# Moving the broadcasts of places from GpSimd's queue to SP's, with the places stored in eight copies

## The reference, cut to what matters

```
h = maximum(layernorm(x), 0)                                  # x: 6250 nodes x 64
x = x + segment_sum(h[src], dst, num_segments=6250)           # 200000 edges, sorted by dst
h = maximum(layernorm(x), 0)
for l in range(3):                                            # second layer: attention masks on the same edges
    mask = clip(sigmoid(mlp(x_l[src], x_l[dst])) * 1.5 - 0.45, 0, 1)
    x_l  = segment_sum(mask * d_inv_sqrt[src] * d_inv_sqrt[dst] * x_l[dst], src)
    out  = out + x_l
```

## Time and profile before

| | |
|---|---|
| time, median of 3 runs | 4300.82 us (4297.33 to 4306.86) |
| the profiled execution: its time | 4298.2 us |
| its span in the trace | 4296.5 us |
| sorting stage, first to last store of bins | 71.8 to 498.2 us |
| building stage, first broadcast issued to the next stage's first instruction | 523.8 to 1153.6 us |
| busy share of the span: PE, DVE, ACT, POOL | 87%, 84%, 46%, 55% |
| bytes moved | 794.22 MB, of these 78.69 MB by GpSimd's queue |

### The profile page before, as it was taken

The page is one execution under the profiler, slowest core; times in us unless marked ns, Lnnn a source line. Parts: engine busy times, 40 slices in busy tenths (PEclk is TensorE's granted clock), DMA queues, the critical chain, the costliest instruction groups (busy, mean ns, idle before and its releaser), DMA issues. The chain is left out here.

```text
span 4296.5 us, 257308 instructions
## 1 busy us (share of the span) xinstructions
PE 3754.2 (87%) x99727; PEld 3555.5 (83%) x99728; DVE 3612.2 (84%) x5865; ACT 1965.7 (46%) x5107; POOL 2355.7 (55%) x3286
## 2 busy tenths in 40 slices
PE   5888678888689999799988999799997999979997
PEld 4777577887569999788868999788885999978887
DVE  8999867787758888899966888799995888879998
ACT  5888767777621111555541111255552111135554
POOL 3777523333223333789962333399894333359987
PEclk8888799999889999899989999899998999989999
DMA  1000189999637776566626777566662777756665
GB/s 31 2 2 2 35 282 327 323 330 321 217 131 248 249 248 225 150 171 171 171 72 217 247 247 247 175 173 171 172 170 79 246 247 247 247 151 170 170 171 138
DMA packets 521189, 794.22 MB, mean 185 GB/s; under 512 B 61718, under 2 KB 461514, under 8 KB 521098
## 3 DMA queue, kind: packets, MB, share of 16 engines
q1 hardware_dynamic: 500714, 714.25, 52.5%
q0 software_dynamic: 20384, 78.69, 6.7%
HBM read 672.34 MB, written 120.42 MB: 185 GB/s over the span
## 5 line engine op out<-in xcount | busy, mean ns | idle before, releaser
L1547 POOL TENSOR_TENSOR message<-message 128x448 f32<-128x448 f32 x1029 | 1244.7, 1242 | 195.9 <-ACT message L1531 195.9
L1243 PE MATMUL pre_ps<-rows_a,hotT_a 128*128 128x64 bf16 x21609 | 1302.6, 194 | 55.0 <-DMA hotT_a<-hot_scratch 27.8
L1243 PE MATMUL pre_ps<-table,hotT_a 128*128 128x64 bf16 x21609 | 1301.7, 194 | 1.8 <-issue 1.8
L1243 PEld LDWEIGHTS pre_ps<-rows_a,hotT_a 128*128 128x128 fp8e4 x21609 | 1130.4, 98 | 81.4 <-issue 64.4
L1243 PEld LDWEIGHTS pre_ps<-table,hotT_a 128*128 128x128 fp8e4 x21609 | 1132.8, 98 | 0.8 <-issue 0.7
L1558 DVE TENSOR_TENSOR message<-message 128x448 f32<-128x448 f32 x1029 | 993.5, 966 | 69.3 <-POOL message L1547 69.3
L1359 DVE SCALAR_TENSOR_TENSOR weighed<-pre_ps,w 128x448 f32<-128x448 f32 x1029 | 642.3, 624 | 279.8 <-PE pre_ps L1243 192.8
L1531 ACT ACTIVATE message<-high_ps,mask 128x64 f32<-128x64 f32 x3087 | 699.7, 326 | 248.2 <-PE high_ps L1490 231.2
L1502 PE MATMUL sum_ps<-message,hot_b 128*128 128x192 bf16 x7203 | 783.9, 247 | 6.1 <-DVE message L1558 5.7
L1490 PE MATMUL low_ps<-table,hot_b 128*128 128x64 bf16 x12348 | 529.3, 193 | 152.9 <-issue 62.4
L1490 PEld LDWEIGHTS low_ps<-table,hot_b 128*128 128x128 fp8e4 x12348 | 473.1, 98 | 195.0 <-issue 181.9
(11 more groups left out here) (160 smaller groups left out, 5142.8 us busy)
## 6 DMA issues: line engine op xcount, KB each, us to landing
hotT_a<-hot_scratch SPq DMA_DIRECT2D x1029, 224.0 KB, 4.5
hot_b<-hot_scratch SPq DMA_DIRECT2D x1029, 224.0 KB, 2.7
hot_scratch<-hot SPq DMA_DIRECT2D x343, 336.0 KB, 7.8
hot_a<-hot_scratch SPq DMA_DIRECT2D x147, 784.0 KB, 5.0
places<-slots_scratch POOLq DMA_DIRECT2D x196, 224.0 KB, 6.8
places<-slots_scratch POOLq DMA_DIRECT2D x98, 336.0 KB, 7.2
out<-res SPq DMA_DIRECT2D x1, 1536.0 KB
slots_scratch<-bins SPq DMA_DIRECT2D x49, 16.0 KB, 1.4
```

The lines of the kernel that those rows point to most:

```text
L1243: last = nc.tensor.matmul(pre_ps[g][:, j, :], hotT[:, b, g, end, j * P:(j + 1) * P].bitcast(FP8), table, start=end + part == 0, stop=end = ...
L1547: pool.tensor_tensor(message[:, g, :, 1, :], message[:, g, :, 0, :], top[:, g, :, 0, :, 1], ALU.subtract).then_inc(s["rest_ready"], 1)
```

## The change

Four things change. The scratch tensor of places becomes eight copies of itself, and the sorting stage stores each block's 16 KB eight times, once into each copy. In the building stage GpSimd issues nothing; SP issues the broadcasts, between its stores: after the store of a chunk's last unit it issues the two loads of that chunk for the row two later, without a wait of its own. The source of a load is now all eight copies of a row, each read by 16 partitions, where before it was the one copy read by 128. And since SP issues loads after every chunk's last unit, also in the last pair of rows, it loads two rows more than before (rows 49 and 50, which no unit reads), and waits for these at the end of the stage.

```diff
-                    act.wait_ge(stored[b], nth * 16)
+                    act.wait_ge(stored[b], nth * (16 * COPIES))
...
-                    sp.dma_start(k.slots_dram[:, bass.ds(c, 1), :].rearrange("r c e -> r (c e)"), bins[:, b, :])\
-                        .then_inc(stored[b], 16)
+                    for copy in range(COPIES):
+                        sp.dma_start(k.slots_dram[copy, :, bass.ds(c, 1), :].rearrange("r c e -> r (c e)"), bins[:, b, :])\
+                            .then_inc(stored[b], 16)
...
+    last_of = {z - 1: c for c, (a, z) in enumerate(chunks)}
...
-            @block.gpsimd
-            def _(pool):
+            @block.sync
+            def _(sp):
                 def load(c, h, r):
                     a, z = chunks[c]
                     for e in range(2):
-                        tile = k.slots_dram[bass.ds(r + e * k.HALF, 1), a * G:z * G, :]
-                        pool.dma_start(places[:, h, e, a * G * P:z * G * P],
-                                       tile.rearrange("r c e -> (r c e)").partition_broadcast(P))\
+                        tile = k.slots_dram[:, bass.ds(r + e * k.HALF, 1), a * G:z * G, :]
+                        n = (z - a) * G * P
+                        sp.dma_start(places[:, h, e, a * G * P:z * G * P],
+                                       tile.rearrange("o r c e -> o (r c e)").unsqueeze(1).to_broadcast([COPIES, P // COPIES, n]))\
                             .then_inc(places_in[c][h], 16)
 
-                for c in range(len(chunks)):
-                    load(c, 1, 0)
-                for c in range(len(chunks)):
-                    load(c, 0, 1)
-                for c, (a, z) in enumerate(chunks):
-                    wait_count(pool, s, s["hotT"], z)
-                    load(c, 1, 2)
-                with pool.Fori(1, (NB - 1) // 2) as i:
-                    for c, (a, z) in enumerate(chunks):
-                        for h in range(2):
-                            wait_count(pool, s, s["hotT"], NG + (i - 1) * (2 * NG) + 2 * (z - 1) + h + 1)
-                            load(c, h, i * 2 + 1 + h)
-
-            @block.sync
-            def _(sp):
                 def store(recent):
                     n = recent[0]
                     wait_count(sp, s, s["hotT"], n.u + 1)
                     wait_count(sp, s, s["hot_ready"], n.u + 1)
                     sp.dma_start(k.hot_dram[bass.ds(n.r, 1), :, n.g, :, :].rearrange("r p a b -> (r p) a b"),
                                  hot[:, n.slot, 0:3, :]).then_inc(stored[n.slot], 16)
+                    if n.g in last_of:
+                        load(last_of[n.g], n.h, n.r + 2)
+
+                for c in range(len(chunks)):
+                    load(c, 1, 0)
+                for c in range(len(chunks)):
+                    load(c, 0, 1)
                 each_unit(sp, k, 1, store)
+                for c in range(len(chunks)):
+                    for h in range(2):
+                        sp.wait_ge(places_in[c][h], 32 * (NB // 2 + 1 + h))
                 for g in range(NG):
                     sp.wait_ge(stored[g], 16 * NB)
...
-    k.slots_dram = nc.dram_tensor("slots_scratch", [2 * k.HALF, k.NB, P], U8).ap()
+    k.slots_dram = nc.dram_tensor("slots_scratch", [COPIES, 2 * k.HALF, k.NB, P], U8).ap()
```

More of the change, by code:

```diff
@@ L16 @@
 PARTS = 3
+COPIES = 8
 CH = 8
@@ L498, in _ @@
                 for b in range(2):
-                    sp.sem_inc(stored[b], 16)
+                    sp.sem_inc(stored[b], 16 * COPIES)
                 def row(c, b, nth, first):
                     wait_count(sp, s, s["bins_ready"], c + 3)
-                    sp.dma_start(k.slots_dram[:, bass.ds(c, 1), :].rearrange("r c e -> r (c e)"), bins[:, b, :])\
-                        .then_inc(stored[b], 16)
+                    for copy in range(COPIES):
+                        sp.dma_start(k.slots_dram[copy, :, bass.ds(c, 1), :].rearrange("r c e -> r (c e)"), bins[:, b, :])\
+                            .then_inc(stored[b], 16)
                 each_row(sp, NB, row)
-                sp.wait_ge(stored[0], 16 * (NB // 2 + 2))
-                sp.wait_ge(stored[1], 16 * (NB // 2 + 1))
+                sp.wait_ge(stored[0], 16 * COPIES * (NB // 2 + 2))
+                sp.wait_ge(stored[1], 16 * COPIES * (NB // 2 + 1))
             @block.vector
```

## The result

The changed kernel takes 4411.74 us (median of 4 runs, 4408.9 to 4414.36), against 4299.61 of the kernel before beside it: a ratio of 1.0258, 95% interval 1.024 to 1.0275. It is slower by 112 us, where +108 was forecast (4409, range 4325 to 4520). The profiled execution has a span of 4408.5 us, 112.0 more than before.

What follows compares the result with a forecast made beforehand. The building stage was taken as bound by the VectorE-TensorE-ScalarE round trip, DMA close behind. Sorting 0, GpSimd 0, SP 0 and building +108 gave 4406 us profiled, 4409 as the median, range 4325 to 4520.

Steps and rivals of the forecast that it cites:

- the round trip of 1.69 us a unit: Building stage: paced by the round trip between VectorE, TensorE and ScalarE, 343 units, 580 us, with DMA close behind.
- Eight engines, the term that decides: Building stage: loads run on always the same eight DMA engines, 17.6 MB each, 738 us against 629.8, +108; chance 0.85.
- The reading of the 106-partition store: Kernel's last store: DMA share 0.16 read as two engines, the number dividing 106, so eight copies give eight engines.
- The price of an engine: Building stage: a busy engine moves 24.0 GB/s, between 22.1 (+171 us) and 26.0 (+51 us).
- The two useless rows: Building stage: two more rows loaded, 3.2 MB over eight engines, 17 us of the 108.
- The seven more stores a block: Sorting stage: eight stores take SP 2.7 us of 8.9 a block, hidden, taken as 0.
- the other end: Sorting stage: the cost of the extra stores, taken as 0, could at its other end be about 1 us.
- GpSimd's issues: Building stage: 294 issues, 211.7 us busy, go from GpSimd; gain 0 to 2 us, taken as 0.
- SP's issue of a load: Building stage: 0.332 us each, 26 issues take 8.6 us of a turn of at least 23.7; SP keeps up, 0.
- VectorE's waits: Building stage, sign of the forecast: VectorE idle for DMA ahead of line 984 some 140 us rather than 34.
- the first one: Building stage rival: all sixteen engines carry the loads and waits for stores go; 4271 us, chance 0.09.
- The third rival: Building stage: sixteen engines but one in-order queue, loads ahead of stores; +27 us, 4328, chance 0.03.

Runs made afterwards that it cites:

- swap16: Changed kernel with the loads' source dimensions exchanged to [16 repeats][8 copies][bytes]; 4283.86 us against 4307.77 for the kernel before, ratio 0.9945.
- sixteen: Changed kernel with sixteen copies in place of eight, copies still outermost; 4281.58 us against 4323.51 for the kernel before, ratio 0.9902.
- stores_only: Kernel before plus the sorting stage's eight stores a block; GpSimd still issues and reads only the first copy; ratio 1.0006 to the kernel before.
- pool_swap: Kernel before with eight copies stored, GpSimd still issuing, all eight read as [16 repeats][8 copies][bytes]; ratio 0.9928 to the kernel before.
- swap16_no_extra: Changed kernel with source dimensions exchanged to [16 repeats][8 copies][bytes] and no two useless rows; ratio 0.9918 to the kernel before, 0.9896 when run again.
- queue_only_no_extra: Changed kernel with one copy, plain broadcast issued by SP, and no two useless rows; 4283.42 us, ratio 0.9911 to the kernel before.
- no_extra: Changed kernel without the two useless rows, SP's last pair issuing no loads; ratio 1.0214 to the kernel before.
- four: Changed kernel with four copies in place of eight, source [4 copies][32 repeats][bytes]; 4776.0 us against 4307.77 for the kernel before, ratio 1.1084.

## Why the prediction was right

**What bounds the kernel.** That the stage runs at the round trip of 1.69 us a unit, with DMA close behind, was right. swap16 has no waits for stores; its 600 to 1100 window has 440 VectorE instructions, finds and adds in a ratio of two to one, so 293 units in 500 us, 1.71 each.

**Eight engines, the term that decides.** Shown by three readings. While broadcasts run alone, from 528 to 531, the share is 0.25 for four engines, 0.48 for eight, and 0.98 and 1.05 for sixteen (sixteen and swap16). The time follows the divisor: 1.1084, 1.0258, and 0.9945 or 0.9902. And exchanging two dimensions of the source, with nothing else touched, takes the loss away. The reading of the 106-partition store carried over to a source whose destination has 128 partitions, though it was thin ground: a share of 0.16 is 2.5 engines, not two.

That the eight are always the same is not seen directly, since no view names an engine. It follows from the share later on:

```profile
600.00:1100.00 500.00, 381.94 (x9970) 365.02 (x9968) 333.41 (x357) 332.08 (x510) 0.00 (x0) 0.91 0.73 273
```

Two fifths of a unit's bytes are places and three fifths its store. Each of a fixed eight then carries 0.4/8 + 0.6/16 = 8.75% of all bytes, and each of the others 3.75%. Eight engines full and eight at 3.75/8.75 = 0.43 make a share of 0.71; 0.73 is measured. With eight that change from load to load every engine would carry the same, and nothing would hold the share down while stores are waited for. The same sum gives 0.45 for four engines, against 0.47. It also answers whether TensorE's lower clock is a cause: with eight engines full all the time, the stage can't be waiting for TensorE. No run holds the clock fixed to show this apart.

**The price of an engine.** 24.0 GB/s was taken between 22.1 and 26. Measured: 17.6 MB in 746.6 - 4 us, 23.7 GB/s over the stage. From 600 to 1100 alone it is 8.75% of 273 GB/s, 23.9. The building stage came to +116.8 us where +108 was forecast. At 23.9 the 17.61 MB take 737 us, so of the 9 us some 3 are the rate, and 6 are the ends of the stage, which take nearly 10 us and not 4. That 24.0 was so close is in part luck. The ground for a faster engine counted two engines in the last store, 17.5 GB/s each; by its share of 0.16 there are 2.5, 14.0 GB/s each, no faster than the 13.6 before it. At 22.1 or 26 the same sum gives 4472 or 4352 us. That the whole came within 3 us is luck as well: the rest of the kernel, which the change doesn't touch, gave 4.8 us back: 1.0 more up to the first broadcast, 5.8 less behind the stage (3142.9 before, 3137.1 after). In the other traces that last part lies anywhere between 3134.7 and 3144.1 us, so it belongs to the execution, not to the change.

**The two useless rows.** Their 17 us were in the sum, but I had placed them nowhere. The trace puts most of them at the end: SP stands 10.8 us when all computing is done. In that wait the last microseconds are slower than eight engines would be:

```profile
1259.00:1269.00 10.00, 0.00 (x0) 0.00 (x0) 0.22 (x1) 0.00 (x0) 0.00 (x0) 0.56 0.34 133
...
1265.00:1268.00 3.00, 0.00 (x0) 0.00 (x0) 0.00 (x0) 0.00 (x0) 0.00 (x0) 0.50 0.10 38
```

A share of 0.10 is as much as one or two engines of sixteen. Most likely these still have work when the others of the eight are done, but the views don't name them. The mean of eight engines is thus a little too kind a measure for the end of the stage.

**Costed at nothing.** The seven more stores a block: stores_only has 1.0006. The first broadcast is issued at 523.3 to 523.8 in the three traces with one copy and at 523.6 to 526.5, mostly near 525, in the eight with eight copies; so about 1.5 us are lost ahead of the stage, near the 1 us named as the other end. SP's part was put too low: stores follow each other by 0.53 us, not by the 0.337 of one issue (the last block's eight start from 499.9 to 503.6), so eight take 4.2 us of 8.9 and sixteen nearly all of it. GpSimd's issues: right that they cost nothing as such, since pool_swap keeps them and can't be told from swap16_no_extra, run with it (0.9928 and 0.9918, the intervals overlap). SP's issue of a load: put at 332 ns from the stores, measured 663, twice too low, with no effect, since SP had room.

**VectorE's waits.** Forecast some 140 us for DMA; measured 113.6 for stores and 9.5 for places, and another 10.5 at the stage's end. With 18.9 us more for `add_up` these are 112 of the stage's 116.8. The landing of stores was to grow over 10 us and is 10.2. GpSimd is busy 259 us less in the page (2355.7 to 2096.5), not 212: 44 of it lie in the sorting stage, where its small operations show other durations and nothing waits for them.

**The rivals.** The price of the first one, 4271 or 30 us less, was nearly right for a kernel that uses all sixteen engines: swap16 is 24 us faster than the kernel before it. One of its grounds was half right. The packets of the software queue do cost more a byte, 43% from 600 to 1100 in the kernel before; in pool_swap, with eight copies read, it is 21%, and the waits for stores are gone. So about half of it went with the single copy (queues from 600 to 1100, the kernel before and pool_swap: packets, MB, share of the engines). On SP's queue the single copy cost no time that could be told.

```profile
q1 hardware_dynamic: 40593, 96.98, 49.7%
q0 software_dynamic: 16640, 64.24, 47.0%
...
q1 hardware_dynamic: 42159, 100.75, 53.2%
q0 software_dynamic: 17286, 66.79, 42.6%
```

The third rival, stores delayed by loads ahead of them in one queue, is refuted by swap16, where a store lands in 5.4 us rather than 7.8.

**A faster version.** swap16_no_extra beats both kernels: 0.9918 (0.9905 to 0.9932) in one set of runs and 0.9896 (0.9881 to 0.9911) in another, 31 to 45 us under the kernel before. queue_only_no_extra, which needs no copies, is at 0.9911 and can't be told from it, and pool_swap, which keeps GpSimd's queue and reads eight copies, is at 0.9928. So either half of the change, the queue or the copies, gives the gain, and both together give little or nothing more.

## What to carry to other kernels

Look at the outermost dimension of both sides of every transfer that SP issues before anything else: with four or eight there, four or eight of sixteen DMA engines carried it here, and a transfer that is itself hardly waited for still delayed another that shares its engines. Put a repeat dimension of sixteen outside and the eight copies inside, or have sixteen copies. When a stage's DMA share falls while its time grows, compare the share with the fraction of engines (0.25, 0.48) in a window in which only the suspected transfer runs. Set the window by the first issue, some 3 us behind it: from 526 to 529 the changed kernel shows 0.44, and no_extra, with the same loads issued 1.3 us later, 0.21.

## What the runs showed of the hardware that was not expected

- On GpSimd's queue a broadcast from one copy to 128 partitions costs about a sixth more of the engines' time than one from eight copies (6.9% of the span in stores_only against 5.9% in pool_swap, for the same 20384 packets), and moved the time by 0.8% (1.0006 against 0.9928). On SP's queue one copy and eight gave the same time (0.9944 and 0.9945) and differed in landing, 6.7 and 5.1 us. While broadcasts run alone it is the other way round on both queues: 366 and 353 GB/s from one copy, 241 and 252 from eight, the engines full in all four (from 528 to 531). Why, and why the two queues differ in time, was not found.
- The same source form, eight outermost, takes eight engines on SP's queue and isn't held to the same eight on GpSimd's (share 0.48 against 0.94 from 528 to 531; 1.0258 against 0.9934).
- SP's issue of a load has a median of 355 ns for one copy, 572 for [16][8], 663 for [8][16] and 1221 for [4][32]. The shortest ones are 332, 537, 596 and 528 ns, so it is the second counting dimension that costs some 200 ns, and not the number of engines. The rest of the long medians may be standing in a full queue, which no run shows.
- An engine moves more with fewer at work. With broadcasts of several copies alone (528 to 531) it is 15.8 GB/s each at sixteen, 18.9 at eight and 22.0 at four (252, 151 and 88 GB/s in swap16, the change and four). With stores among them, from 600 to 1100, it is 20.9, 23.9 and 25.2, where at sixteen the pace is set by the round trip and not by DMA.
